# The five orders of the local layers, written out anew

## What is computed

```
h = layernorm(x)*(1+ca)+sa ;  x = x + ga * causal_attention(h)        # 16 heads of 64
h = layernorm(x)*(1+cb)+sb ;  y = h
for i in range(6):
    y = local_attention(shift(y), Wqkv[i], q_scale[i], k_scale[i], Wo[i]) + y
    y = ffn(shift(y), ln_g[i], ln_b[i], W1[i], b1[i], W2[i], b2[i]) + y
x = x + gb * y
```

## Time and profile before

| | |
|---|---|
| median of 3 runs | 3508.06 us (3505.7 to 3515.55) |
| span of the profiled execution | 3495.1 us (its own time is not given; the median is 13.0 more) |
| instructions | 158019 |
| TensorE busy | 3309.7 us (95%) |
| VectorE busy | 2951.4 us (84%) |
| GpSimd busy | 2907.1 us (83%) |
| ScalarE busy | 2468.4 us (71%) |
| granted TensorE clock | 0.986 of 2.4 GHz |
| copies of keys (kf<-h), from issue to landing | 2.5 us median |

### The profile page before, as it was taken

How to read it: one execution, slowest core, us unless ns; L and a number is a source line. 1 busy time by engine, 2 the same in 40 slices (tenths; PEclk the granted TensorE clock), 3 DMA queues, 4 the chain that set the end, 5 groups by cost and what they waited for, 6 DMA issues and landing times.

```text
span 3495.1 us, 158019 instructions
## 1 busy us (share of the span) xinstructions
PE 3309.7 (95%) x69988; PEld 1936.2 (55%) x69988; DVE 2951.4 (84%) x3104; ACT 2468.4 (71%) x3349; POOL 2907.1 (83%) x2483
## 2 busy tenths in 40 slices
PE   7999999779999999999999999999999999999997
PEld 4666666445555555555555555555555555555553
DVE  6888888688888988888888889888998889988873
ACT  5777777556777767777677777676877777767764
POOL 3665555588999989999899999898999999989993
PEclk9999999999999999999999999999999999999997
DMA  1000000154645545545455454555554554545452
GB/s 67 5 5 5 5 5 5 44 119 102 143 114 130 120 115 126 131 112 127 113 126 127 106 137 110 129 120 121 120 135 105 142 124 109 140 108 134 102 124 62
DMA packets 163861, 347.33 MB, mean 99 GB/s; under 512 B 32876, under 2 KB 42352, under 8 KB 153840
## 3 DMA queue, kind: packets, MB, share of 16 engines
q1 hardware_dynamic: 163184, 337.23, 40.9%
HBM read 24.62 MB, written 4.19 MB: 8 GB/s over the span
## 4 chain that ended last, share of the span: by engine, by line
PE 70%; DVE 11%; POOL 6%; issue 6%; ACT 4%; SPq 2%; DMA 1%; DVEq 0%; POOLq 0%; ACTq 0%
PE psA L697 29%; PE psB L697 23%; PE psB L559 8%; PE psA L559 6%; PE psB L754 3%; DVE h L1338 3%; DVE pt L1237 1%; SPq L490 1%; PE psA L754 1%; DVE negm L1342 1%; DVE sum L1349 1%; DVE ts L1330 1%; DVE h L1320 1%; DMA kf<-h 1%; POOL sq L1443 1%
## 5 line engine op out<-in xcount | busy, mean ns | idle before, releaser
L1410 POOL TENSOR_TENSOR pt<-wk,pt 128x256 f16<-128x256 f32 (+3 forms) x256 | 368.1, 1455 | 288.7 <-ACT pt L939 199.0
L1443 POOL TENSOR_TENSOR sq<-sq 128x512 f32<-128x512 f32 x384 | 488.5, 1281 | 79.6 <-ACT sq L1022 78.2
L1438 POOL TENSOR_TENSOR h<-h,ts 128x512 f32<-128x512 f32 x384 | 499.8, 1302 | 1.2 <-DVE ts L1330 1.2
L1439 POOL TENSOR_TENSOR h<-h,ts 128x512 f32<-128x512 f32 x384 | 497.1, 1295 | 0.0
L1338 DVE TENSOR_TENSOR h<-h,psB 128x1024 f32<-128x1024 f32 x288 | 337.8, 1215 | 57.1 <-PE psB L697 55.5
L1463 POOL TENSOR_TENSOR pb<-pb,rc 128x1024 f32<-128x1024 f32 x192 | 366.3, 1908 | 8.8 <-DVE rc L1351 8.8
L1320 DVE TENSOR_TENSOR h<-psA,t_rot 128x1024 f32<-128x1024 f32 x192 | 234.2, 1220 | 72.7 <-ACT sq L1022 65.7
L697 PE MATMUL psA<-kf,qf 64*32 64x64 f32 x18432 | 251.2, 224 | 22.0 <-issue 21.6
L697 PEld LDWEIGHTS psA<-kf,qf 64*32 64x32 f32 x18432 | 191.5, 106 | 124.8 <-issue 124.4
L1320 DVE TENSOR_TENSOR h<-psB,t_rot 128x1024 f32<-128x1024 f32 x192 | 233.4, 1216 | 26.2 <-ACT sq L1022 20.4
L1022 ACT ACTIVATE sq<-psA 128x1024 f32<-128x1024 f32 x192 | 197.0, 1027 | 63.7 <-PE psA L697 63.5
(11 more groups left out here) (368 smaller groups left out, 10242.0 us busy)
## 6 DMA issues: line engine op xcount, KB each, us to landing
qf<-h SPq DMA_DIRECT2D x768, 136.0 KB
kf<-h SPq DMA_DIRECT2D x768, 136.0 KB, 2.5
vev<-vo SPq DMA_DIRECT2D x288, 256.0 KB
vev<-vo SPq DMA_DIRECT2D x96, 192.0 KB
stage<-wqk SPq DMA_DIRECT2D x24, 256.0 KB, 5.0
stage<-wvl SPq DMA_DIRECT2D x12, 256.0 KB, 4.1
stage<-wof SPq DMA_DIRECT2D x12, 256.0 KB, 5.5
xb<-xt SPq DMA_DIRECT2D x8, 256.0 KB, 7.9
```

The lines of the kernel that those rows point to most:

```text
L1410: e.tensor_tensor(pt[g][pr][:, :, 1, o:o + w], wk[(slot_of(s)[0] - 1) % SLOTS][:, :, 0:w], pt[g][pr][:, :, 0, o:o + w], ALU.subtract).then ...
L1438: e.tensor_tensor(halves_of(h, 0), halves_of(h, 0), t[1], ALU.subtract)
L1439: e.tensor_tensor(halves_of(h, 1), halves_of(h, 1), t[0], ALU.add).then_inc(ended["ad"])
L1443: e.tensor_tensor(sqb[c][:, 0, :], sqb[c][:, 0, :], sqb[c][:, 1, :], ALU.add).then_inc(ended["qa"])
```

## The change

All five strings are replaced. The multiset of steps of each string is the same (57, 55, 54, 32 and 14 tokens), so no instruction is added or removed; their order, the rounds ahead, and the PSUM places differ.

The second part: on VectorE the two products of a rotation may now come in either order (`ts01` before `tc01`, for instance), so the last reader of a `pj` is no longer always `ts`, and that of `la` no longer always `lw`. `take` asks `later` which of the two comes last.

```
-TENSOR: pv000:B+1 ng10+1 pv001+1 ss1:Dl+1 sc110:A+1 tp01:C+1 sc113+1 sc111+1 sc112+1 pj00:B+2 pv010:D+1 ng11+1 pv011+1
-  vp10:C+1 fo:Bl tp10:C+1 vp11:A+1 bc11:B+1 bc10:C+1 f2:D+1 f0:A+1 pv100:C+1 pv101+1 pj01:D+2 tp11:B+1 pj02:A+2
-  pj03:C+2 pv110:B+1 f1:D+1 pv111+1 sc000:A+2 ss0:Dl+2 sc002+2 sc001+2 pj10:D+2 sc003+2 op:Bl+1 sc010:C+2 bc00:D+2
-  ng00+2 vp01:B+2 sc012+2 sc013+2 sc011+2 bc01:D+2 la:Br+2 pj11:A+2 ng01+2 pj12:B+2 vp00:D+2 tp00:C+2 sc100:A+2
-  pj13:D+2 sc102+2 sc103+2 sc101+2 lb:C+2
+TENSOR: tp00:D+3 sc100:A+3 sc101+3 sc102+3 sc103+3 pj13:B+3 lb:C+3 pv000:D+3 pv001+3 ng10+3 tp01:B+3 sc110:C+3 ss1:Al+3
+  pj00:B+4 sc111+3 sc112+3 sc113+3 vp10:A+3 ng11+3 pv010:D+3 pv011+3 fo:Br+2 tp10:C+3 vp11:A+3 bc10:C+3 bc11:B+3
+  f2:D+3 f0:A+3 pv100:C+3 pv101+3 pj01:D+4 tp11:B+3 pj02:A+4 pv110:B+3 pj03:C+4 f1:D+3 pv111+3 sc000:A+4 ss0:Dr+4
+  sc003+4 sc002+4 pj10:D+4 sc001+4 op:Br+3 sc010:C+4 bc00:D+4 sc012+4 sc011+4 sc013+4 ng00+4 vp01:B+4 ng01+4 pj11:A+4
+  bc01:D+4 la:Bl+4 pj12:C+4 vp00:B+4
-GPSIMD: gl1 lx+1 nw1+1 pn10+1 cs1+1 fl+1 ct1+1 xl+2 ad13+1 pn11+1 qa00+2 ad00+2 qa01+2 qa02+2 qa03+2 ad01+2 ad02+2 gl0+1
-  nw0+2 cs0+2 ct0+2 ad03+2 qa10+2 ad10+2 pn00+2 qa11+2 qa12+2 ad11+2 pn01+2 qa13+2 ad12+2 gl2+1
+GPSIMD: fl+4 ct1+4 pn11+4 ad13+4 ad00+5 qa00+5 gl2+4 qa01+5 qa02+5 xl+5 qa03+5 ad01+5 ad02+5 nw0+5 cs0+5 ct0+5 qa10+5 ad10+5
+  ad03+5 pn00+5 gl0+4 qa11+5 ad11+5 gl1+4 qa12+5 pn01+5 qa13+5 ad12+5 lx+5 nw1+5 pn10+5 cs1+5
-VECTOR: ... sm11+2 ol01+2 fr+1 ow1+1 wl11+2 bm10+2 bm11+2 bm12+2 fm2+2 ws0 bm13+2 fm0+2 ...
+VECTOR: ... sm11+3 ol01+3 fr+2 ws0+1 bm10+3 bm11+3 bm12+3 fm2+3 bm13+3 fm0+3 ow1+2 wl01+4 ol10+3 ts01+4 tc01+4 ...
+VECTOR: ... wf0+1 wl02+3 tc03+3 mx00+3 tc10+3 ts10+3 rs+2 bm01+3 mx01+3 bm00+3 sm00+3 bm02+3 bm03+3 ts11+3 tc11+3 tc12+3 ...
-SCALAR: ... wh10+1 lr+1 ex10+1 oe00+1 nr1+1 wh00+2 ns1 te01 sq00+1 wh12 ex11 fh oe01 ca1 ve10 cb1 te10 ve11 ge2 ge0 oe10 ...
+SCALAR: ... oh1+2 lr+3 oe00+3 ex10+3 te01+3 oh0+2 nr1+3 ns1+3 sq00+4 xh+4 wh12+3 ex11+3 fh+3 ca1+3 oe01+3 wh01+4 ve10+3 ...
-SYNC: st6 st7 dm00+1 dm01+1 dm02+1 dm03+1 st5+1 vd0+1 dm10+1 dm11+1 st4+2 dm12+1 dm13+1 vd1+1
+SYNC: st4+6 st7+5 dm10+5 dm11+5 dm12+5 dm13+5 vd1+5 st5+6 st6+6 dm01+6 dm00+6 dm03+6 dm02+6 vd0+6
-LAST = {"tp": "te", "op": "rs", "pj": "ts", "ss": "nr", "vp": "ve", "la": "lw", ...
+LAST = {"tp": "te", "op": "rs", "ss": "nr", "vp": "ve", "lb": "ln", "f": "fm", "fo": "fr"}
+        def later(steps, a, b):
+            return max(a, b, key=steps.index)
...
+                    elif k == "pj":
+                        e.wait_ge(*done(*later(vector_walk, ("tc", *at), ("ts", *at))))
+                    elif k == "la":
+                        e.wait_ge(*done(*later(scalar_walk, ("lq", *at), ("lw", *at))))
```

More of the change, by code:

```diff
@@ L126 @@
 TENSOR = (
[5 rows of a table removed]
[5 rows of a table added]
 )
 SCALAR = (
[3 rows of a table removed]
[4 rows of a table added]
 )
 VECTOR = (
[4 rows of a table removed]
[4 rows of a table added]
 )
 GPSIMD = (
-    "gl1 lx+1 nw1+1 pn10+1 cs1+1 fl+1 ct1+1 xl+2 ad13+1 pn11+1 qa00+2 ad00+2 qa01+2 qa02+2 qa03+2 ad01+2 ad02+2 gl0+1 "
-    "nw0+2 cs0+2 ct0+2 ad03+2 qa10+2 ad10+2 pn00+2 qa11+2 qa12+2 ad11+2 pn01+2 qa13+2 ad12+2 gl2+1 "
+    "fl+4 ct1+4 pn11+4 ad13+4 ad00+5 qa00+5 gl2+4 qa01+5 qa02+5 xl+5 qa03+5 ad01+5 ad02+5 nw0+5 cs0+5 ct0+5 qa10+5 ad10+5 "
+    "ad03+5 pn00+5 gl0+4 qa11+5 ad11+5 gl1+4 qa12+5 pn01+5 qa13+5 ad12+5 lx+5 nw1+5 pn10+5 cs1+5 "
 )
 SYNC = (
-    "st6 st7 dm00+1 dm01+1 dm02+1 dm03+1 st5+1 vd0+1 dm10+1 dm11+1 st4+2 dm12+1 dm13+1 vd1+1 "
+    "st4+6 st7+5 dm10+5 dm11+5 dm12+5 dm13+5 vd1+5 st5+6 st6+6 dm01+6 dm00+6 dm03+6 dm02+6 vd0+6 "
 )
@@ L152 @@
 NEXT = ("ca", "cs", "cb", "ct", "pj", "sq", "tc", "ts", "ad", "ss", "nr", "ns", "nw", "bc", "bm", "vp", "ve", "vd", "qa", "dm")
-LAST = {"tp": "te", "op": "rs", "pj": "ts", "ss": "nr", "vp": "ve", "la": "lw",
-        "lb": "ln", "f": "fm", "fo": "fr"}
+LAST = {"tp": "te", "op": "rs", "ss": "nr", "vp": "ve", "lb": "ln", "f": "fm", "fo": "fr"}
 def walk(text):
```

## The result

The kernel after takes 3547.1 us (median of 4 runs, 3540.54 to 3555.01), the kernel before, run beside it, 3511.8 us (3505.70 to 3518.58). The ratio is 1.010, 95% interval [1.007, 1.013]: slower by 35 us where 36 us less had been forecast. It lies outside the range, and its interval is clear of no change.

What follows compares the result with a forecast made beforehand. TensorE was taken to set the pace. Saving 0.9 us less 0.15 a round gives 0.75, or 36 us over 48 rounds: span 3495.1 falls to 3459, plus 13.0 for the median makes 3472 us, range 3444 to 3514.

Steps and rivals of the forecast that it cites:

- issue stalls: TensorE's idle time named "issue" in the profile before: 28.9 us in 1800 us, 0.9 us a round.
- missing instructions: Rival: three newly unbroken runs of scores and values each stall 0.7 us a round; net +0.45, 22 us, 3530; chance 0.14.
- mean rate over 10 us: Argument against more issue stalls: `pj13` and `lb` stand between two dense runs, so TensorE's mean instruction rate stays.
- Tile shapes: TensorE's changes of matmul shape fall from 39 to 34 a round, 0.10 us each: 0.5 us a round saved.
- `ss`: Both sums of squares on TensorE now follow scores, where they start sooner than behind `pv`: 0.2 us a round less.
- `vp00`: Its standing TensorE wait for PSUM place D goes, as it takes B: 0.2 us a round less, nothing if ScalarE's copy is late.
- VectorE and ScalarE "nothing": Same work reordered, four places with under 0.4 us to spare: nothing in the sum, 0.5 us a round for the range.
- GpSimd: Second normalisation ends 2.3 us later, so TensorE waits 0.4 to 0.5 us at `tp01` in one round; 0.15 taken on average.
- A ceiling of 54.8 a round: Shortest round in us that GpSimd's work permits, 0.8 under the round taken apart and 1.8 under the average.
- DMA "nothing": SyncE's reordered copies land in time, first scores coming over 5 us after their product against 2.5 needed: nothing.
- Layer changes: `pv100` waits 2.3 us behind `ws0`, replacing 2.7 before `tp11`: nothing in the sum, 3 us a layer either way.
- signs named for "wrong": Issue stalls over 45 us in 1800; TensorE behind `ts`, `otl` or `ptb`; rounds over 56.4; a layer change over 8 us.

Runs made afterwards that it cites:

- E6: Kernel after, idle TensorE instructions holding its 256-instruction block ends at position 208 (instructions from last block end to end of `ss1`); 3620.8 us, 1.032 to before.
- E1: Kernel before with copies of queries, keys and shifted values cut to one partition each, local attention not computed; 3474.2 us, 0.992 to before.
- E2: Kernel after with copies of queries, keys and shifted values cut to one partition each, local attention not computed; 3451.1 us, 0.985 to before.
- E5: Kernel after, idle TensorE instructions holding its 256-instruction block ends at position 102 (instructions from last block end to end of `ss1`); 3476.2 us, 0.991 to before.
- E15: Kernel after, idle TensorE instructions holding its 256-instruction block ends at position 80 (instructions from last block end to end of `ss1`); 3530.0 us, 1.004 to before.
- E7: Kernel before, idle TensorE instructions holding its 256-instruction block ends at position 98 (instructions from last block end to end of `ss1`); 3535.3 us, 1.008 to before.

## Why the prediction was wrong

By its own steps:

- *The sum has no term for issue stalls that grow.* This is the step that failed. They were carried on as 0.9 us a round; they became 1.85. The rival "missing instructions" names the kind, the three runs and the sign, and its 0.45 a round for the net loss compares with 35 us over 48 rounds, 0.73. It was given 0.14 and argued down with `pj13` and `lb` between the runs and the "mean rate over 10 us". What decides is no mean rate but one block of 256 instructions against the start of the next one's fetch and 2.5 us, and its ends lie where the count puts them. The rival has the kind right and the place only in part: of the 44 us of added stalls 39 stand behind blocks of 3.6 us or more and 26 lie at `pv100`, a run that was unbroken before.
- *No term for the clock.* The prediction read 1.00 and left it there. Behind long stalls it falls to 1.2 GHz: 75 us of the local layers after, 27 before, by the estimate above 0.5 a round.
- *The page.* The Trainium skill says of the fetch of blocks that it is "mostly hidden" (Runtime: NRT & Kernel Launch, Instruction fetch mechanics). Here the trace does not agree: issue stalls, nearly all of them at block ends, are 46 us in the kernel before, 90 after and 146 in E6. The prediction saw that 28.9 us spoke against it and did not ask where they lay; counting the instructions between stalls would have shown it.
- *Tile shapes, `ss`, `vp00`: 0.9.* The standing wait before `vp00` no longer shows. Of the 63 waits read as "mostly this one" 31 were (17 of 31 us); the other 32 stood before a weight load of `pv`, and 31 such (23 us) are there after. The stretches between waits are 0.4 a round shorter, not 0.9, where stalls are few (E1, E2), and not shorter where they are many, since the lower clock takes it back.
- *VectorE and ScalarE "nothing".* `tc11` before `sc100` was seen and put in the shade of a wait at `tp01` that hardly exists; it costs 14.3 us in 1800, 0.45 a round. With `tp01` behind `tc13` (0.18) it is the second failed step. Named waits together grew by 0.45.
- *GpSimd.* `pb` at `tp01`: 0.15 forecast, one wait of 0.4 us. A ceiling of 54.8 a round: E5's two rounds run at 54.9 and 54.4, so it was about right, and never reached by the kernel itself.
- *DMA "nothing".* Right for copies that arrive too late, wrong for what they do on the way: with the copies small the kernel after wins some 90 us (E2).
- *Layer changes.* 2.3 us behind `ws0` forecast, 2.4 measured.
- Of the signs named for "wrong", three came: issue over 45 (56.0), rounds over 56.4, TensorE behind `otl` (3.5 us).

What is worth keeping: the new order with its ends at position 102 (E5) takes 3476 against 3507 beside it and beats both kernels. At 24 us of stalls the new order leads by 0.7% (E1, E2), at 75 to 80 (E15, E7) by 0.4%; what the new order gains is real and smaller than what the block ends took.

## What to carry to other kernels

Before trusting an order of many small matmuls, count TensorE's instructions, mark every 256th, and ask how long each block lasts and when the fetch of the next one starts; when the stalls named issue lie at one remainder, a few idle instructions at the right count can be worth more than a reordering (here 145 us between two positions). Compare orders at their best position, or with the drift averaged, and find the position by trying: it can't be read from neighbours. Tight waits may be the end of a loop through a copy: follow what the waiting step itself waits for before moving it.

## What the hardware showed that I had not expected

- The first instruction of a stalled block runs 2.3 to 2.9 us after its fetch starts though the packet takes 1.1, and the fetch does not start until 1.0 (copies small) to 1.2 us (whole) after the block before is entered.
- Some fetches start 3 to 7 us after the block before is entered, at places that recur from round to round, with copies running or not (E15, E1). Late ones make most of the stalls that the change added: 48 us against 5. Why they start late is open.
- A stall of 1.3 to 2.1 us in a busy TensorE can bring the lower clock behind it: 13 times in the kernel after. From E5 to E6 123 us more of stalls went with 165 us more time.
